# A fused kernel of conditional layers on one core: another order of the opening, of the half-block sums and of the work at quarter boundaries

## What is computed

```python
x = x + einsum('bct,bcd->bdt', x, W0[subject])
x = x + einsum('bct,bcd->bdt', x, W1[adapter])
x = x + einsum('bct,bcd->bdt', x, W2[adapter]) + bias[adapter][:, :, None]
# a feed-forward block over the 512 columns, hidden width 2048, with low-rank adapters (rank 16)
gate = x @ Wg + (x @ Ag[adapter]) @ Bg[adapter]
up   = x @ Wu + (x @ Au[adapter]) @ Bu[adapter]
h    = silu(gate) * up
x    = x + h @ Wd + (h @ Ad[adapter]) @ Bd[adapter]
```

## Time and profile before

| | us |
|---|---|
| median of 3 runs (lowest, highest) | 1345.57 (1345.12, 1346.62) |
| the profiled execution, its own time | 1347.3 |
| its span, first to last instruction | 1345.5 |
| TensorE busy | 1316.3 |
| VectorE busy | 994.4 |
| GpSimd busy | 629.4 |
| ScalarE busy | 549.2 |

### The profile page before, as it was taken

One profiled execution on the slowest core, in us unless ns is written; L12 is line 12 of the kernel. 1 busy time (PEld: TensorE's weight loads), 2 busy tenths in 40 slices (PEclk: granted clock), 3 DMA queues, 4 the chain that ended last, 5 costly groups with the idle time before them and its releaser, 6 DMA issues.

```text
span 1345.5 us, 17990 instructions
## 1 busy us (share of the span) xinstructions
PE 1316.3 (98%) x6402; PEld 1095.5 (81%) x6402; DVE 994.4 (74%) x1530; ACT 549.2 (41%) x940; POOL 629.4 (47%) x531
## 2 busy tenths in 40 slices
PE   8699999999999999999999999999999999999998
PEld 7478888888888888888888888888887888888886
DVE  5776688777787667788678767777877876777765
ACT  3444444444334335444334334444433334433331
POOL 2256565455405545555431655554542444444440
PEclk8799999999999999999999999999999999999999
DMA  4445354445636334555383534444446432333321
GB/s 168 157 136 198 109 176 141 153 142 165 232 148 211 122 102 132 158 169 150 113 316 114 184 103 144 147 150 130 152 176 250 153 98 83 106 99 114 114 78 63
DMA packets 105687, 197.00 MB, mean 146 GB/s; under 512 B 10368, under 2 KB 54656, under 8 KB 105600
## 3 DMA queue, kind: packets, MB, share of 16 engines
q1 hardware_dynamic: 83328, 125.06, 28.6%
q0 software_dynamic: 22272, 70.80, 16.3%
HBM read 160.69 MB, written 35.13 MB: 146 GB/s over the span
## 4 chain that ended last, share of the span: by engine, by line
PE 88%; DVE 6%; DMA 1%; POOL 1%; issue 1%; ACT 1%; SPq 0%; ACTq 0%; DVEq 0%; POOLq 0%
PE px L1104 26%; PE pd L1104 25%; PE py L1104 12%; PE pz L1104 6%; PE pv L1104 6%; PE pz L1120 4%; PE py L1120 2%; PE px L1120 2%; PE pd L1322 2%; DMA w_raw<-w_gu 1%; DVE wg_lo L844 1%; PE pd L1131 1%; DVE h_lo L1006 1%; DVE acc L1001 1%; PE pd L1177 1%
## 5 line engine op out<-in xcount | busy, mean ns | idle before, releaser
L496 POOL DMA_INDIRECT b_got<-b_table,idx_b x256 | 257.4, 1006 | 288.2 <-PE py L1120 204.5
L514 POOL TENSOR_TENSOR h_lo<-g,h_hi 128x512 fp32r<-128x512 f32 x128 | 176.4, 1378 | 334.0 <-ACT h_hi L586 332.8
L977 DVE TENSOR_TENSOR acc<-pd,acc 128x512 f32<-128x512 f32 x256 | 174.7, 690 | 82.1 <-PE pd L1104 81.7
L1104 PE MATMUL px<-xo_hi,wg_hi 128*128 128x512 f32 x544 | 222.9, 410 | 11.8 <-ACT g L586 5.7
L586 ACT ACTIVATE wg_hi<-w_raw 128x512 fp32r<-128x512 f32 (+1 forms) x272 | 155.6, 573 | 169.6 <-PE py L1120 94.5
L844 DVE TENSOR_TENSOR wg_lo<-w_raw,wg_hi 128x512 fp32r<-128x512 f32 (+1 forms) x272 | 198.1, 733 | 34.6 <-ACT wg_hi L586 33.8
L1104 PE MATMUL px<-xo_hi,wg_lo 128*128 128x512 f32 x544 | 213.5, 392 | 0.0
L1104 PE MATMUL px<-xo_lo,wg_hi 128*128 128x512 f32 x544 | 213.5, 392 | 0.0
L1104 PE MATMUL pd<-wd_hi,h_hi 128*128 128x512 f32 x512 | 203.1, 397 | 1.0 <-POOL h_lo L514 0.9
L1104 PE MATMUL pd<-wd_lo,h_hi 128*128 128x512 f32 x512 | 199.4, 389 | 0.0
L1104 PE MATMUL pd<-wd_hi,h_lo 128*128 128x512 f32 x512 | 199.3, 389 | 0.0
(11 more groups left out here) (213 smaller groups left out, 2327.2 us busy)
## 6 DMA issues: line engine op xcount, KB each, us to landing
w_raw<-w_gu SPq DMA_DIRECT2D x68, 512.0 KB, 3.7
wd_raw<-w_dn SPq DMA_DIRECT2D x64, 320.0 KB, 3.0
xo_hi<-xops SPq DMA_DIRECT2D x21, 512.0 KB, 8.2
xo_lo<-xops SPq DMA_DIRECT2D x21, 512.0 KB, 9.9
acc<-x SPq DMA_DIRECT2D x8, 1024.0 KB, 8.3
out<-acc SPq DMA_DIRECT2D x7, 1024.0 KB, 4.6
xops<-st_hi SPq DMA_DIRECT2D x24, 256.0 KB, 2.8
xops<-st_lo SPq DMA_DIRECT2D x24, 256.0 KB, 2.9
```

The costliest lines, as they stand in the source:

```text
L496: gp.indirect_dma_start(out=dst, out_offset=None, in_=rows_of, in_offset=bass.IndirectOffsetOnAxis(ap=rows.bitcast(U32), axis=0)).then_inc ...
L514: return gp.tensor_tensor(dst, src_raw, src_hi, ALU.subtract)
L977: ins = dve.tensor_tensor(dst, pd[j][:, :], dst, ALU.add)
L1104: ins = pe.matmul(psum, w_parts[wi], x_parts[xi], start=(start and i == 0), stop=(stop and i == 2), skip_group_check=more)
```

## The change

It changes the order in which instructions stand in the lists, two queues, and the number of `warm_up` matmuls; nothing is computed differently.

1. SyncE's opening: the adapter numbers and the bias are issued from ScalarE's queue. SyncE waits for the numbers, w2 and w1, then loads w_raw; waits for four one-hot matrices, then loads x; waits for `oe_add`, then loads b_rows.
2. VectorE's opening: one one-hot matrix is made ahead of `oe_add` instead of four; the first weight sums and low parts, the low part of b_rows and the indexes change places; `selectors(0, 0)` goes behind the low parts of A11 and A12.
3. TensorE's opening: `o_combine(0)` goes ahead of the last two selections; two of the second group's turns go ahead of the first product; WARM_UP goes from (10, 14, 10), of which the third number is used nowhere, to (8, 1, 9, 4), with nine matmuls ahead of the S1 product and four ahead of the S2 product of the first unit.
4. ScalarE's opening: the sums px and py of the first unit are kept between the operand conversions, not behind them all.
5. Units -1 and 0 on VectorE: two of the four weight sums go behind the addition that sets `u3_done`; in unit 0 the second group of low parts goes behind three additions; in unit -1 the whole `select(q, 0)` goes ahead of the four additions of `finish`, and the last group of low parts behind them.
6. Unit 1 on ScalarE: the down weights are converted, and the next unit's first weights too, only after all three sums are kept.

The core of the diff:

```diff
-WARM_UP = (10, 14, 10)
+WARM_UP = (8, 1, 9, 4)
...
             sp.dma_start(ints[:, 0, :], subject.partition_broadcast(P)).then_inc(ints_in, 16)
-            sp.dma_start(ints[:, 1, :], adapter.partition_broadcast(P)).then_inc(ints_in, 16)
             sp.dma_start(w2_four, w2_rows.rearrange("p (j n) -> p j n", j=TP)).then_inc(e0_in, 16)
             sp.dma_start(w1_four, w1_pairs.rearrange("p (j n) -> p j n", j=TP)).then_inc(e0_in, 16)
-            sp.dma_start(bias_src, bias_pairs).then_inc(bias_in, 16)
+
+            sp.wait_ge(ints_in, 2 * 16)
+            sp.wait_ge(e0_in, 2 * 16)
+            load_weights(0)
+            sp.wait_ge(pick_made, TP)
             load_x(0, 0)
-            load_weights(0)
             load_x(0, 1)
+            sp.wait_ge(oe_add, 1)
             load_b(0)
-            sp.wait_ge(oe_add, 1)
...
+            act.dma_start(ints[:, 1, :], adapter.partition_broadcast(P)).then_inc(ints_in, 16)
+            act.dma_start(bias_src, bias_pairs).then_inc(bias_in, 16)
...
                 copy(xo_hi[:, k, :], s_raw[k]).then_inc(o_hi[k], 1)
-            copy(xo_hi[:, A22, :], a2_raw[1]).then_inc(o_hi[A22], 1)
+                if k == S1:
+                    keep_s1(0)
+                    copy(xo_hi[:, A22, :], a2_raw[1]).then_inc(o_hi[A22], 1)
+                if k == S2:
+                    keep_s5(0)
+                if k == S3:
+                    keep_s2(0)
...
+                if b % 2 and b > 1:
+                    down_highs(q, b)
...
-                if not last and b > 0:
+                if not last and b > 1:
                     weights_high(n + 1, 0)
...
+                if n:
+                    keep_s2(n)
+                if b == 1:
+                    down_highs(q, b)
+                if not last and b <= 1:
                     weights_high(n + 1, 0)
...
-            for p in range(TP):
-                picks(p)
+            picks(0)
             dve.wait_ge(e2_done, 1)
             dve.wait_ge(oe_mm, 1)
             dve.tensor_tensor(es_four[:, :, C:2 * C], four(pv[:, 0:TP * C]), e2_four, ALU.add).then_inc(oe_add, 1)
-            for p in range(TP, QP - 1):
+            for p in range(1, TP + 2):
                 picks(p)
+            sums(0)
             picked(0)
-            picks(QP - 1)
-            sums(0)
+            for p in range(TP + 2, QP):
+                picks(p)
             dve.wait_ge(eb_done, 1)
             o_combine(0)
-            picked(1)
-            block_numbers()
             for g in (0, 2, 1, 3):
                 weights_low(0, g)
+            picked(1)
+            b_low(0)
+            block_numbers()
             dve.wait_ge(eb_done, 2)
             o_combine(1)
-            b_low(0)
...
                 if not last and b <= 0:
 
-                    sums(n + 1)
+                    first_sums(n + 1)
...
                 dve.tensor_tensor(up1[:, :], px[:, :], up1[:, :], ALU.add).then_inc(u3_done, 1)
+                if not last and b <= 0:
+                    second_sums(n + 1)
...
                     ua_low(q, 1, 1, 3)
                     weights_low(n + 1, 2)
-                    weights_low(n + 1, 3)
                     ua_low(q, 1, 0, 4)
-                    if q:
-                        finish(q - 1, 0, range(0, 2))
                     select(q, 0)
                     if q:
-                        finish(q - 1, 0, range(2, TP))
+                        finish(q - 1, 0)
+                    weights_low(n + 1, 3)
                     selectors(q, 1)
...
+            picked(range(TP + 2))
+            o_combine(0)
+            picked(range(TP + 2, QP))
+            o_layers(0)
             pe.wait_ge(bias_done, 1)
-            o_combine(0)
-            o_layers(0)
             o_combine(1)
...
+                if first:
+                    for a in range(2):
+                        first_turn(a)
...
+                    pe.wait_ge(o_a2_kept, TP)
+                    warm_up(WARM_UP[2], pv)
...
+                if first:
+                    warm_up(WARM_UP[3], pv)
```

More of the change, by code:

```diff
@@ L1055, in _ @@
                     weights_low(n + 1, 0)
-                if not last and behind:
+                if not last and behind and b:
                     weights_low(n + 1, 1)
@@ L1123, in lora, with warm_up @@
                 return ins
[L1125 removed]
+            def warm_up(count, psum=px):
                 for _ in range(count):
[L1127 removed]
+                    pe.matmul(psum[:, 0:P], ident[:, :], ident[:, :], start=True, stop=True)
             def turn(par, t, j, psum):
@@ L1265, in _ @@
                 if first:
-                    for a in range(TP):
+                    for a in range(2, TP):
                         first_turn(a)
```

69 lines of the change are left out of this document (39 added, 30 removed).

## The result

The changed kernel takes 1350.78 us (median of 7 runs, 1349.89 to 1353.43) where the kernel before takes 1345.57 (7 runs): a ratio of 1.0038, 95% interval 1.0027 to 1.0050. It is **slower by 5.2 us**; 11.6 us less had been forecast. The profiled execution took 1353.43 with a span of 1351.6, 6.1 above the 1345.5 of before.

The account below looks back on a forecast made before the run. TensorE, busy 1316.3 of 1345.5 us, was taken as the bound, leaving only the opening and quarter boundaries to win. Terms -6.9 - 0.9 - 0.6 - 3.2 = -11.6 gave a median of 1334.0 us, range 1329 to 1340.

Parts of the forecast that it names:

- A: Start to the second group's layers (31.39): these start at 24.5, between 23.2 and 27.1; -6.9 us (-8.2 to -4.3).
- A at -5.4: Opening, if the skill's rule holds and the new queue saves only the issuing time: total time 1335.6 us.
- the selections and the first combination took 8.1 us, and this stays: Opening on TensorE: they start at about 9.0 and keep their length, so the first group's layers could start at 17.1.
- a stretch of 3.3 us lost: Opening: if the clock falls in TensorE's wait from 5 to 6.7 us, the selections lose 3.3 us, giving 26.5.
- B: Second group's layers to unit 0 (64.00): shorter waits give -4.2 us, a clock fall costs 3.3; -0.9 us.
- C: Units 0 and 1, first quarter: waits for silu and kept px shrink or go; -0.6 us (-2.2 to 0).
- GpSimd's h_lo, named as the next wait: Units 0 and 1, first quarter: TensorE's down matmuls next wait for it, giving back any gain beyond about 0.5 us.
- D: Three quarter boundaries: waits for up (2.2 us) and u (1.0 us) go; -3.2 us (-3.2 to -2.2).
- up's -2.2: Three quarter boundaries: TensorE's wait for up goes, as ScalarE keeps px before the conversion that waits for late weights.
- a landing 0.6 us after VectorE wants it: Boundaries: w_raw, issued 4.8 us later, lands at 395.9, wanted at 395.3; the 0.6 falls into slack on TensorE.
- Slower: late weights at the boundaries: Rival: w_raw takes 9.5 us to land, costing 5.4 us at each of three boundaries; 1350.2 us, chance 0.03.
- the chance of 0.94 for faster: Whole kernel: faster by more than 2.7 us, from the forecast's 0.60 and two rivals' 0.14 and 0.20.

Follow-up runs that it names:

- open_14: Kernel before with only the change's opening, and 14 warm-up matmuls instead of 1 ahead of the selections: 1343.24 us against 1345.57, ratio 0.9980.
- b_split: Kernel before with only VectorE's four weight sums cut in two, the two second ones behind the u3 addition: 1351.97 us against 1346.51, ratio 1.0044.
- b_keep2: Kernel before with only ScalarE's s2 kept ahead of the next unit's weights in unit 1, down conversions unmoved: 1342.18 us against 1345.57, ratio 0.9970.
- b_select: Kernel before with only unit 0's selection ahead of the finished tokens and the last group's low parts behind both: 1347.78 us against 1346.51, ratio 1.0015.
- bound_only: Kernel before with only items 5 and 6 of the change (units -1, 0 and 1), opening unchanged: 1353.98 us against 1346.5, ratio 1.0062.

## Why the prediction was wrong, step by step

- **A, the opening to 31.39: -6.9 forecast, +1.4 measured.** The queueing part held in direction: the first useful matmul moved from 8.62 to 7.30, 1.3 us where I took 1.9, the selections started at 9.99 (forecast 9.0), and ScalarE did not wait for b_rows past 24 (it had them at 22.6). The adapter numbers landed after 4.1 us, not 5.6, but the subject's after 4.6, not 3.6. Even the 1.3 is in part luck of the two executions: over all profiles that matmul starts at 8.06 to 8.62 with the old queues (nine kernels, median 8.15) and at 7.21 to 7.77 with the new ones (nine, median 7.53), 0.6 apart. That is nearer the 0.4 that the prediction worked out beside the rule of the Trainium skill (DMA: Bandwidth & Descriptors, section on issuing engines not being separate DMA queues) than the 1.9 that it took. (With A at -5.4 the forecast's own sum gives 1335.5, not 1335.6.) What failed is "the selections and the first combination took 8.1 us, and this stays". They took 15.2 us (9.99 to 25.24). I had priced the clock as a stretch of 3.3 us lost, and saw in the 14 warm-ups only matmuls to be saved. What they were there for was in the earlier trace rows: clock 0.55 while they ran, full rate behind them. open_14, with fourteen of them back, has the layers of the second group at 27.68, 5.1 us ahead of the changed kernel.
- **B, to unit 0: -0.9 forecast, -2.3 measured.** Here the mechanism was right: TensorE stood idle 4.4 us ahead of the selecting matmuls, and they and unit 0's first product ran at half rate. Why the stretch came out 1.4 us shorter than forecast, behind layers that came 8 us later than forecast, no run separates.
- **C, units 0 and 1: -0.6 forecast, +2.2 measured.** The half rate lasted into unit 0 (six matmuls in 2.6 us instead of 1.4, 1.2 us), which I had booked wholly under B; GpSimd's h_lo, named as the next wait, cost 1.2 us, more than the two waits for g and silu gave back (1.0), and waits for up (0.4) and u (0.3) came in.
- **D, the boundaries: -3.2 forecast, +4.8 measured.** The step that failed is the one that wasn't taken: the split of the sums has no price in the forecast, which doesn't ask who waits in place for the two second sums and what is queued behind that. b_split puts it at 5.5 us over the whole run, 3.2 of them at the boundaries by its posts. Of the two waits that I did follow, up's -2.2 was right in direction for keeping px early alone (b_keep2: -3.4), but I let the down conversions go at nothing because nobody needs them for 8 us; what they delay is behind them and beside them. For the selection I had computed the late load rightly (4.8 us later; b_select has 717.14 where the kernel before has 712.29), and a landing 0.6 us after VectorE wants it. It was there after some 4.2 us, not 3.7, the first sum came at 721.36 instead of 720.06, 1.3 late, and the slack on TensorE that I counted on wasn't there: it waited 1.1 us for u.
- **The rivals.** "Slower: late weights at the boundaries" named one of the two places, with a price of 5.4 a boundary where it is about 1.3; alone it would not have made the kernel slower. The cause that did, an in-place wait ahead of h_hi, was in no case, so the chance of 0.94 for faster rested on a list that wasn't complete.

## What to carry to other kernels

When an operation is moved later, look up who waits for it and then what stands behind that waiter in its own list: the price is there, even if the waiter itself is in no hurry; and moving those instructions ahead of the waiter takes the price away (5.5 us to 0.9). Before taking warm-up matmuls out, price the stretch behind them at both clock levels, and read the level from durations of like matmuls, not from the clock column alone. Compare a post with those of several profiles of the same code: here one execution's opening differed from another's by up to 2.1 us. Time each piece of a many-part reordering alone: here two orders inside the change are gains by themselves (1.9 and 3.4 us), hidden by what was moved along with them.

## What the hardware showed that was not expected

TensorE was busy without a gap from 7.3 to 28 us in the changed kernel, mostly with 128x64 matmuls, and stayed at half rate (16 records in 3.52 to 3.62 us) all that time; with 28 records of 128x128 ahead of them the same matmuls ran at the full rate (1.90 to 1.95). The engine was busy and the clock column said 1.00 throughout, and still the lower level was in force. At 390 us a TensorE that had been busy 2.89 of 4 us dropped to 0.50 for 3.4 us; in bound_only it had been busy 2.90 of the same 4 us and stayed at 1.00, and what decides between them no run here shows. And a 128x512 subtraction of VectorE took 1.01 to 1.47 us instead of 0.68, and a 128x256 one 1.28 to 1.61 instead of 0.41, while GpSimd did the same kind of work beside it.
